# Attention over two batches: query pieces scaled once and copied by transfers between partitions, the own weights' product in front of the first factor's

## The chip, the cores and the metric

One core of a Trainium2 chip runs the whole program. The metric is the device time of one launch in microseconds. The engines are TensorE (PE in the profile), VectorE (DVE), ScalarE (ACT), GpSimd (POOL) and SyncE (SP), which here only issues transfers. "Q" behind an engine's name (SPq, ACTq) means its queue of transfers or its sequencer.

## The reference

The network has three layers. Only the first is touched here:

```python
# x: (32, 64, 512)  ctx: (32, 1601, 512), float32
hc = layernorm(x)                    # 64 tokens a batch
w1, w2, w3 = w_sim[:512], w_sim[512:1024], w_sim[1024:]
Sim = (hc @ w1)[:, :, None] + (ctx @ w2)[:, None, :] \
    + einsum('bid,bjd->bij', hc * w3, ctx) + b_sim
A = softmax(Sim, axis=2)
hq_hat = einsum('bij,bjd->bid', A, ctx)
Batt = softmax(max(Sim, axis=2), axis=1)
hc_bar = einsum('bi,bid->bd', Batt, hc)[:, None, :]
feats = concat([hc, hq_hat, hc * hq_hat, hc * hc_bar], -1)
x = x + feats @ W_qv + b_qv          # W_qv: (2048, 512)
...                                  # a recurrence, then a layer of 8 experts
```

So the query of a token is `hc * w3 + w2`, and a score is its product with a row of the context. The term `hc @ w1` is the same for all context rows of a token, and is dropped from the softmax.

## The kernel before

The attention takes 16 pairs of batches: two batches of 64 tokens make 128 partitions. `bodies` runs a first step (front only), 15 full steps and a last one (back only). A full step with index p does the back of pair p (values, features, output) and the front of pair f = p + 1 (queries, scores, exponentials). Every engine runs its own copy of the step in a written order, and the engines meet only at semaphores.

TensorE's order in a full step (`body` at L447):

- `values`: 13 context positions, the probabilities against the context rows, into the PSUM bank `O`, two column halves (one for each batch). Behind position n = 1 `spread_queries` for two of four blocks; behind n = 5 a small product that spreads `brow` (the softmax over tokens) over all partitions, into `Y`. At n = 1 also the turn of `tcol`.
- `spread_queries` for the other two blocks, then the turn of `tok_rows` (hq_hat) into the bank `T[0]`, which waits for ScalarE to empty `O` (L545).
- the first factor, `product(hqT, 0, ...)`, L408, with w12's first four chunks; it waits for ScalarE's copy `hqT` (L548).
- `own_product`, L416, chunks 0 and 1: hc against weights that depend on the batch, `w0 + w3 * hcb`. GpSimd makes these (`own_weights`, L326 and L329: for each chunk two multiplications and two additions), in two buffers by turns.
- `scores`, L401: 16 blocks of 32 channels, 128 multiplications, four row groups by two column halves at a time, so a block's 32 channels lie in one row group. It needs all context turned (`turned`) and all queries (`q_ready`).
- the second factor `f3` (L408) and own chunks 2 and 3, the turns of the probabilities, the turn of the next pair's tokens.

The layout of the scores asks for each block of 32 query channels at each of the four row groups of 32 partitions. The tokens' transpose `hcT` has channel block e of chunk c on the partitions of group e only. `spread_queries` multiplies it with `spread`, four identity blocks side by side, which copies block e to all four groups, in the PSUM bank `S[:, e]`. ScalarE then scales the copies into `qr` (`queries`, L522): 16 pieces of 128 by 128 for each pair, with `w3R` and `w2R`, columns that hold each block's 32 weights four times. `qr` lies in a part of `x2`, which is not used yet.

VectorE turns the context in 32 by 32 blocks into `ctxT` (L609, L627): the six positions of `ctx_two` one pair ahead, the seven of `ctx_one` in four parts as their transfers land. Between them it does the softmax over tokens (L655 to L670), and `hcb` (L679 and L683), which waits for the brow product. SyncE issues the parts' loads as `values` sets each buffer free (`av_one`), and the two big loads behind its end (`av_done`).

Of the kernel before, what the change touches and what calls it, by code (L numbers as in the profile page):

```python
# [14 lines left out]
P = 128  # L15
# [36 lines left out]
Q = 32  # L52
# [33 lines left out]
def later(p, n):  # L86

    return not isinstance(p, int) or p >= n


def cross_attention(nc, sh, ident, x, ctx, w_sim, b_sim, W_qv, b_qv, x1, x2, ahead):
# [5 lines left out]
    with ExitStack() as stack:  # L97
        def sb(name, shape, dt=F32):
            return stack.enter_context(nc.sbuf_tensor(name, shape, dt))
# [7 lines left out]
        ctx_one = [sb(f"ctx_one{b}", [P, ONE, D]) for b in range(2)]  # L107
        qr = x2[:, 2 * TWO:2 * TWO + C, :].rearrange("p c (e i) -> p (c e) i", e=QUADS)
        w0, w3 = sb("w0", [P, C, D]), sb("w3", [P, C, D])
# [13 lines left out]
        bqv_b = sb("bqv_b", [P, D])  # L123
        spread = sb("spread", [P, P])
        w2R = sb("w2R", [P, DB])
        w3R = sb("w3R", [P, DB])
        bsim_b = sb("bsim_b", [P, 1])
# [29 lines left out]
        wqv_in, w12_in = sem("wqv_in"), sem("w12_in")  # L157
        spread_ready = sem("spread_ready")
        hqT_ready = sem("hqT_ready")
# [12 lines left out]
        xb_ready = sem("xb_ready")  # L172
        q_full, q_ready = sem("q_full"), sem("q_ready")
        hcT_full, hcT_ready = sem("hcT_full"), sem("hcT_ready")
# [51 lines left out]
        def _(sp):  # L226
# [18 lines left out]
            sp.dma_start(w1_b[:], bcast_row(w_sim[0:D])).then_inc(const_in, 16)  # L245
            with nc.allow_non_contiguous_dma(reason="two small weight vectors, a column for each block of 32"):
                for a in range(QUADS):
                    rows = slice(a * Q, (a + 1) * Q)
                    sp.dma_start(w2R[rows, :], w_sim[D:2 * D].rearrange("(k s) -> s k", s=Q)).then_inc(const_in, 16)
                    sp.dma_start(w3R[rows, :], w_sim[2 * D:3 * D].rearrange("(k s) -> s k", s=Q)).then_inc(const_in, 16)  # L250
            sp.dma_start(bsim_b[:], bcast_row(b_sim)).then_inc(const_in, 16)
# [51 lines left out]
        def _(pool):  # L303
# [46 lines left out]

            pool.wait_ge(const_in, 176)
            power(0)
# [3 lines left out]
        def _(pe):  # L356
# [29 lines left out]

            def spread_queries(f, fs, blocks):

                pe.wait_ge(hcT_ready, f + 1)
                for e in blocks:  # L390
                    rows = slice(e * Q, (e + 1) * Q)
                    pe.matmul(S[:, e, :], spread[rows, :], hcT[fs][rows].rearrange("p c i -> p (c i)"),  # L392
                              start=True, stop=True).then_inc(q_full, 1)

            def scores():

                for k in range(DB):
                    for a in range(QUADS):
                        tiles = JT if a * Q < JTAIL else JT - 1
                        for b in range(2):  # L400
                            last = pe.matmul(S[64 * b:64 * b + 64, a, 0:tiles * Q], qr[a * Q:(a + 1) * Q, k, 64 * b:64 * b + 64],  # L401
                                             ctxT[a * Q:(a + 1) * Q, 0:tiles, b, k, :], start=(k == 0), stop=(k == DB - 1))
                return last

            def product(lhsT, w, chunks, start):

                for c in chunks:
                    last = pe.matmul(Y[:], lhsT[:, c, :], w12[:, w + c, :], start=start and c == 0, stop=(w > 0 and c == C - 1))  # L408
                return last

            def own_product(p, s, chunks):

                for c in chunks:
                    pe.wait_ge(wb_ready, 2 * (C * p + c + 1))
                    for b in range(2):
                        last = pe.matmul(Y[64 * b:64 * b + 64, :], hcT[s][:, c, 64 * b:64 * b + 64], wb[:, c % 2, b, :],  # L416
                                         start=False, stop=False)
                    last.then_inc(wb_used, 1)

            def values(p, s, step):  # L420

                pe.wait_ge(hqh_ready, p)
                for n, pos in enumerate(AV_ORDER):
                    for q in range(len(AT_TILES)):
                        if AT_TILES[q][0] == n:
                            pe.wait_ge(t_free[(q + 1) % 2], turn((q + 1) % 2, f"probs{q}", *before(p)) + 1)
                    if n == 2 and step != "last":
                        spread_queries(p + 1, 1 - s, (0, 1))
                    if n == 1:
                        pe.wait_ge(tcol_ready, p + 1)  # L430
                        fill(1, "trow", p, step)
                        pe.transpose(T[1][0:1, 0:P], tcol[:], ident[:]).then_inc(t_full[1], 1)
# [12 lines left out]
                last.then_inc(av_done, 1)  # L445

            def body(p, s, step, loads):  # L447
# [4 lines left out]
                if back:  # L452
                    values(p, s, step)
                    if front:
                        spread_queries(f, fs, (2, 3))
                    pe.wait_ge(hqh_ready, p + 1)
                    turn_tile(0, "hqh", tok_rows, p, step)
                    if first(p):
                        pe.wait_ge(w12_in, 16)
                    pe.wait_ge(hcb_step, p + 1)  # L460
                    pe.wait_ge(hqT_ready, p + 1)
                    product(hqT, 0, range(C), True)
                    own_product(p, s, range(half))
                else:
                    pe.wait_ge(spread_ready, QUADS)
                    turn_tokens(f)
                    spread_queries(f, fs, range(QUADS))
                if front:
                    pe.wait_ge(turned, len(PARTS_ONE) * (f + 1))
                    pe.wait_ge(q_ready, DB * (f + 1))  # L470
                    scores().then_inc(qk_done, 1)
                if back:
                    pe.wait_ge(t_free[0], turn(0, "hqh", p, step) + 1)
                    product(f3, C, range(half), False)
                    own_product(p, s, range(half, C))
# [3 lines left out]
                if back:  # L479
                    product(f3, C, range(half, C), False).then_inc(y_done, 1)  # L480
                if front:
# [20 lines left out]
        def _(act):  # L502
# [13 lines left out]

            def queries(f, e):

                act.wait_ge(q_full, QUADS * f + e + 1)
                for c in range(C):  # L520
                    k = c * QUADS + e
                    act.activation(qr[:, k, :], S[:, e, c * P:(c + 1) * P], ACT.Identity,  # L522
                                   scale=w3R[:, k:k + 1], bias=w2R[:, k:k + 1]).then_inc(q_ready, 1)

            def body(p, s, step, loads):
# [50 lines left out]
                if loads is not None:  # L576
                    tokens(f + 1, s if back else 1)

            for e in range(QUADS):
                rows = slice(e * Q, (e + 1) * Q)  # L580
                act.copy(spread[rows, :].rearrange("p (a s) -> p a s", a=QUADS),
                         ident[rows, None, rows].to_broadcast([Q, QUADS, Q])).then_inc(spread_ready, 1)
            act.wait_ge(const_in, 176)
            norm(0)
# [3 lines left out]
        def _(dve):  # L588
            copy = nc.vector.tensor_copy
            dve.wait_ge(const_in, 176)  # L590

# [1699 lines left out]
```

## Time and profile before

| | |
|---|---|
| median of 3 runs | 1359.72 us (1355.3 to 1359.99) |
| profiled execution, its own time | 1357.04 us |
| its span | 1355.3 us |
| TensorE busy | 1232.2 us, 91% |
| VectorE busy | 730.2 us, 54% |
| GpSimd busy | 707.6 us, 52% |
| ScalarE busy | 337.1 us, 25% |
| attention, first to last pair | to about 680 us of the span |

The span is that of one execution on the chip. A line of a timeline has the start in the span, the time from start to end of the merged instructions, the engine, the line of the kernel, what is written from what, and the number of instructions; one float32 multiplication is recorded as two. In square brackets stands the idle time ahead and what ended it. A duration includes latency: for a run of multiplications the distance from start to start tells what each costs.

### The profile page before, as it was taken

What the parts mean: (1) busy time and instruction counts of PE and PEld (TensorE: products, weight loads), DVE (VectorE), ACT (ScalarE), POOL (GpSimd) and SP (SyncE); (2) the same over time, 40 slices, a digit from 0 to 9 for tenths busy, and PEclk for the clock granted to TensorE, in tenths of its full rate; (3) what the DMA queues carried; (4) which work ended last, traced back from release to release, by engine and by line L of the source; (5) the groups of instructions that cost most, each with busy time, mean ns of one, the idle gap of its engine ahead of it and who ended that gap; (6) DMA issues with size and microseconds to landing.
All of it is one profiled execution on the core that took longest, in us unless ns stands there. A gap on an engine that the chain in (4) does not pass through costs nothing. (4 is left out here: it accounts for less than half of the span.)

```text
span 1355.3 us, 29581 instructions
## 1 busy us (share of the span) xinstructions
PE 1232.2 (91%) x10417; PEld 733.4 (54%) x10418; DVE 730.2 (54%) x1573; ACT 337.1 (25%) x768; POOL 707.6 (52%) x762
## 2 busy tenths in 40 slices
PE   0899999999999999999989699999499999999994
PEld 0444434444443444443457456565378888888883
DVE  4555566555566655566259657777733323323325
ACT  2222233232233232233135211111311111111110
POOL 1055544345543445553139656787398553550872
PEclk9999999999999999999979899999599999999997
DMA  8645554434555444555054567863314443321556
GB/s 284 226 146 200 211 209 154 152 145 176 209 209 178 139 153 159 208 210 193 19 191 142 152 204 273 282 208 103 101 51 144 155 155 131 125 100 56 154 161 188
DMA packets 99376, 225.45 MB, mean 166 GB/s; under 512 B 14152, under 2 KB 30664, under 8 KB 95216
## 3 DMA queue, kind: packets, MB, share of 16 engines
q1 hardware_dynamic: 87872, 189.46, 40.9%
q0 software_dynamic: 10288, 33.57, 7.4%
q10 hardware_dynamic: 1152, 1.57, 0.4%
q8 instruction: 40, 0.66, 0.2%
q14 instruction: 24, 0.20, 0.0%
HBM read 179.21 MB, written 45.35 MB: 166 GB/s over the span
## 5 line engine op out<-in xcount | busy, mean ns | idle before, releaser
L326 POOL TENSOR_TENSOR wb<-w,hcb 128x512 f32<-128x512 f32 x120 | 122.1, 1038 | 315.2 <-DVE hcb L683 292.9
L401 PE MATMUL S<-ctxT,x 32*64 32x416 f32 (+1 forms) x4096 | 185.2, 511 | 15.9 <-DVE ctxT L627 15.9
L401 PEld LDWEIGHTS S<-ctxT,x 32*64 32x64 f32 x4096 | 108.5, 133 | 94.8 <-issue 45.8
L329 POOL TENSOR_TENSOR wb<-wb,w 128x512 f32<-128x512 f32 x120 | 150.0, 1271 | 0.0
L609 DVE STREAM_TRANSPOSE ctxT<-ctx_one 128x1024 f32<-128x1024 f32 (+1 forms) x128 | 115.1, 949 | 13.5 <-DMA ctx_one<-in_ctx_dram 13.2
L436 PE MATMUL O<-ctx_one,probsT 128*64 128x512 f32 (+1 forms) x448 | 110.4, 608 | 0.0
L1929 POOL TENSOR_TENSOR w_low<-w_low,w_high 128x2048 fp32r<-128x2048 f32 x21 | 96.7, 4607 | 1.7
L522 ACT ACTIVATE x<-S,w2R,w3R 128x128 f32<-128x128 f32 x256 | 92.7, 472 | 19.5 <-PE S L392 19.5
L2114 DVE TENSOR_TENSOR f_hL<-f_TH,f_hH 128x512 fp32r<-128x512 f32 x39 | 27.0, 692 | 120.4 <-ACT f_hH L2067 117.3
L634 DVE TENSOR_REDUCE mx<-S 128x1 f32<-128x832 f32 x16 | 16.4, 1025 | 128.1 <-PE S L401 128.1
L1452 PE MATMUL Pb<-WrT,yT 128*32 128x128 f32 x2016 | 69.8, 280 | 13.7 <-DVE yT L1705 13.1
L1473 PE MATMUL Wb<-WoT,yT 128*128 128x512 f32 x128 | 71.8, 643 | 0.0
L2072 ACT ACTIVATE sg<-f_G 128x512 f32<-128x512 f32 x39 | 23.3, 597 | 194.1 <-PE f_G L2014 194.1
L408 PE MATMUL Y<-w,hqT 128*128 128x512 f32 x128 | 58.7, 601 | 12.3 <-ACT hqT L548 12.3
L1452 PEld LDWEIGHTS Pb<-WrT,yT 128*32 128x32 f32 x2016 | 52.3, 111 | 28.5 <-DVE yT L1705 25.7
L2012 PE MATMUL f_Dn<-w_high,f_hH 128*128 x156 | 64.2, 412 | 2.3 <-DVE f_hL L2114 1.6
L2012 PE MATMUL f_U<-w_high,f_xH 128*128 x156 | 64.9, 416 | 0.0
L2012 PE MATMUL f_G<-w_high,f_xH 128*128 x156 | 61.7, 395 | 3.2 <-DVE f_xL L2108 3.2
L1947 POOL CAST w_high<-w_low 128x2048 fp32r<-128x2048 f32 x21 | 39.9, 1898 | 42.9 <-DMA w_low<-_L_ffn_gate_up_proj_dram 22.7
L596 DVE BATCH_NORM_STATS2 stats<-x_sb 128x6 f32<-128x512 f32 x16 | 11.1, 693 | 94.9 <-DMA x_sb<-in_x_dram 82.5
L416 PE MATMUL Y<-wb,hcT 128*64 128x512 f32 x256 | 62.0, 605 | 0.0
L408 PE MATMUL Y<-w,f 128*128 128x512 f32 x128 | 62.0, 606 | 0.0
(286 smaller groups left out, 2497.6 us busy)
## 6 DMA issues: line engine op xcount, KB each, us to landing
ctx_one<-in_ctx_dram SPq DMA_DIRECT2D x64, 512.0 KB, 4.5
x<-in_ctx_dram SPq DMA_DIRECT2D x16, 1536.0 KB
ctx_two<-in_ctx_dram SPq DMA_DIRECT2D x16, 1536.0 KB, 9.4
ctx_one<-in_ctx_dram SPq DMA_DIRECT2D x64, 256.0 KB, 5.5
w_low<-_L_ffn_gate_up_proj_dram POOLq DMA_DIRECT2D x10, 1024.0 KB, 8.1
f_xt<-routed_x SPq DMA_DIRECT2D x39, 256.0 KB
routed_y<-f_yt SPq DMA_DIRECT2D x39, 256.0 KB
w_low<-_L_ffn_gate_up_proj_dram SPq DMA_DIRECT2D x6, 1024.0 KB, 8.0
```

The lines of the kernel that those rows point to most:

```text
L326: pool.tensor_tensor(wb[:, slot, b], w3[:, c], hcb[:, c, b, None].to_broadcast([P, D]), ALU.mult).then_inc(wb_step, 1)
L329: pool.tensor_tensor(wb[:, slot, b], wb[:, slot, b], w0[:, c], ALU.add).then_inc(wb_ready, 1)
L401: last = pe.matmul(S[64 * b:64 * b + 64, a, 0:tiles * Q], qr[a * Q:(a + 1) * Q, k, 64 * b:64 * b + 64], ctxT[a * Q:(a + 1) * Q, 0:tiles, b ...
L408: last = pe.matmul(Y[:], lhsT[:, c, :], w12[:, w + c, :], start=start and c == 0, stop=(w > 0 and c == C - 1))
L416: last = pe.matmul(Y[64 * b:64 * b + 64, :], hcT[s][:, c, 64 * b:64 * b + 64], wb[:, c % 2, b, :], start=False, stop=False)
L436: last = pe.matmul(O[64 * b:64 * b + 64, :], probsT[0:rows, n, 64 * b:64 * b + 64], src[0:rows, i, :], start=(n == 0), stop=(n == JT - 1))
L522: act.activation(qr[:, k, :], S[:, e, c * P:(c + 1) * P], ACT.Identity, scale=w3R[:, k:k + 1], bias=w2R[:, k:k + 1]).then_inc(q_ready, 1)
L609: return dve.transpose(ctxT[:, pos:pos + n, b], src[:, i:i + n, :].rearrange("p t (k r) -> p t k r", r=Q))
L1452: last = pe.matmul(Pb[o * B:(o + 1) * B, 0:P], src[:, c, prev, :], WrT[:, c, o * P:(o + 1) * P], start=(c == 0), stop=(c == C - 1))
L1473: last = pe.matmul(Wb[s][:], yT[s][:, c].rearrange("p t b -> p (t b)"), WoT[:, c, :], start=(c == 0), stop=(c == C - 1))
L1929: pool.tensor_tensor(low, low.bitcast(F32), high[:, e % SLOTS, part].bitcast(F32), ALU.subtract).then_inc(w_parts, 1)
L2012: pe.matmul(bank[:], aH[:, c, :], high[:, slot, part, c, :], start=(c == 0), stop=False)
```

## The change

- `spread`, `spread_queries`, their semaphores and the columns `w2R` and `w3R` go. ScalarE scales the turned tokens directly, in the bank `S[:, 3]`, four pieces of 128 by 128 for each pair (`queries`), into a new tile `q3`, with the columns `w2c` and `w3c` (a column for each chunk). It does so at the end of the step before, behind the copy `hcT`.
- A new function `replicate` has ScalarE issue 16 transfers of 32 partitions by 2 KB from `q3` to `qr`: block e to row group a. It stands behind the exponential of `erow`, ahead of the emptying of `O`. `qr` is laid out with e ahead of c, and the scores index it so and wait for the transfers (`q_in`) in place of `q_ready`.
- In a full and the last step, own chunks 0 and 1 are multiplied ahead of the first factor's product, and open the sum in `Y`.
- The brow product is behind position n = 4, no longer n = 5.
- The eight loads for `w2R` and `w3R` at the start become two.

```diff
             def own_product(p, s, chunks):
...
-                                         start=False, stop=False)
+                                         start=c == 0, stop=False)
...
-                    if n == 2 and step != "last":
-                        spread_queries(p + 1, 1 - s, (0, 1))
...
-                    if n == 5:
+                    if n == 4:
...
                 if back:
                     values(p, s, step)
-                    if front:
-                        spread_queries(f, fs, (2, 3))
                     pe.wait_ge(hqh_ready, p + 1)
                     turn_tile(0, "hqh", tok_rows, p, step)
...
                     pe.wait_ge(hcb_step, p + 1)
+                    own_product(p, s, range(half))
                     pe.wait_ge(hqT_ready, p + 1)
-                    product(hqT, 0, range(C), True)
-                    own_product(p, s, range(half))
+                    product(hqT, 0, range(C))
...
                     pe.wait_ge(turned, len(PARTS_ONE) * (f + 1))
-                    pe.wait_ge(q_ready, DB * (f + 1))
+                    pe.wait_ge(q_in, 16 * QUADS * QUADS * (f + 1))
                     scores().then_inc(qk_done, 1)
...
-            def queries(f, e):
-
-                act.wait_ge(q_full, QUADS * f + e + 1)
+            def queries(f):
+
+                if later(f, 1):
+                    act.wait_ge(q_in, 16 * QUADS * QUADS * f)
                 for c in range(C):
-                    k = c * QUADS + e
-                    act.activation(qr[:, k, :], S[:, e, c * P:(c + 1) * P], ACT.Identity,
-                                   scale=w3R[:, k:k + 1], bias=w2R[:, k:k + 1]).then_inc(q_ready, 1)
+                    act.activation(q3[:, c, :], S[:, QUADS - 1, c * P:(c + 1) * P], ACT.Identity,
+                                   scale=w3c[:, c:c + 1], bias=w2c[:, c:c + 1]).then_inc(q_ready, 1)
+
+            def replicate(f):
+
+                act.wait_ge(q_ready, C * (f + 1))
+                if later(f, 1):
+                    act.wait_ge(qk_done, f)
+                for e in range(QUADS):
+                    for a in range(QUADS):
+                        act.dma_start(qr[a * Q:(a + 1) * Q, e], q3[e * Q:(e + 1) * Q]).then_inc(q_in, 16)
...
                 else:
                     tokens(f, 0)
+                    queries(f)
                 if front:
-                    if later(f, 1):
-                        act.wait_ge(qk_done, f)
-                    queries(f, 0)
-                    queries(f, 1)
+                    replicate(f)
...
-                if front:
-                    queries(f, 2)
-                    queries(f, 3)
...
                 if loads is not None:
                     tokens(f + 1, s if back else 1)
+                    queries(f + 1)
```

## Rows read from the trace of the kernel before

**Rows 1.** The page's part 1: busy time, share of the span and instructions.
```profile
PE 1232.2 (91%) x10417; PEld 733.4 (54%) x10418; DVE 730.2 (54%) x1573; ACT 337.1 (25%) x768; POOL 707.6 (52%) x762
```

**Rows 2.** Timeline, TensorE, one pair: start us, us, engine, line, out<-in, count, idle before.
```profile
299.95 1.08 PE L436 MATMUL O<-ctx_one,probsT 128*64 128x512 f32 x4
...
300.96 1.13 PE L392 MATMUL S<-hcT,spread 32*128 32x512 f32 x4
...
302.02 3.65 PE L436 MATMUL O<-ctx_one,probsT 128*64 128x512 f32 x16
...
305.61 0.48 PE L444 MATMUL Y<-brow,ones 1*128 1x128 f32 x2
...
312.18 1.13 PE L392 MATMUL S<-hcT,spread 32*128 32x512 f32 x4
...
313.24 0.66 PE L365 MATMUL T<-ident,tok_rows 128*128 128x128 f32 x4
...
314.66 3.67 PE L408 MATMUL Y<-w,hqT 128*128 128x512 f32 x8 [0.77 <-ACT hqT L548]
...
318.27 1.94 PE L416 MATMUL Y<-wb,hcT 128*64 128x512 f32 x8
...
320.13 11.42 PE L401 MATMUL S<-ctxT,x 32*64 32x416 f32 x256
...
340.19 1.08 PE L436 MATMUL O<-ctx_one,probsT 128*64 128x512 f32 x4
```

**Rows 3.** The same timeline, VectorE and GpSimd on the own weights.
```profile
302.41 2.35 DVE L609 STREAM_TRANSPOSE ctxT<-ctx_two 128x1024 f32<-128x1024 f32 x2
...
306.13 0.69 DVE L679 TENSOR_TENSOR f<-hcT,Y 128x512 f32<-128x512 f32 x1 [1.37 <-PE Y L444]
...
306.94 0.69 DVE L683 TENSOR_REDUCE hcb<-f 128x8 f32<-128x512 f32 x1
...
307.80 2.04 POOL L326 TENSOR_TENSOR wb<-w,hcb 128x512 f32<-128x512 f32 x2 [18.88 <-DVE hcb L683]
...
314.25 2.50 POOL L329 TENSOR_TENSOR wb<-wb,w 128x512 f32<-128x512 f32 x2
```

**Rows 4.** The same timeline, ScalarE's pieces and who takes erow.
```profile
302.12 2.90 ACT L522 ACTIVATE x<-S,w2R,w3R 128x128 f32<-128x128 f32 x8 [1.13 <-PE S L392]
...
312.30 0.69 ACT L545 ACTIVATE tok_rows<-O,rz 128x512 f32<-128x512 f32 x1 [7.28 <-PE O L436]
...
340.93 0.31 ACT L531 ACTIVATE erow<-erow 1x128 f32<-1x128 f32 x1 [1.25 <-DVE erow L658]
...
341.98 0.23 DVE L665 TENSOR_REDUCE rsum<-erow 1x2 f32<-1x128 f32 x1
```

**Rows 5.** Timeline of the kernel's end, ScalarE's transfer issues.
```profile
1340.56 13.02 ACTq L1884 DMA_DIRECT2D out_dram<-x  x24
```

**Rows 6.** Windows of one pair: busy (instructions) per engine; last PEclk, DMA share, GB/s.
```profile
309.00:311.00 2.00, 2.00 (x12) 0.72 (x10) 1.65 (x2) 0.00 (x0) 2.00 (x2) 1.00 0.91 291
...
315.00:317.00 2.00, 2.00 (x6) 0.87 (x5) 2.00 (x4) 2.00 (x7) 2.00 (x3) 1.00 1.02 436
```

**Rows 7.** The pair's timeline: SyncE's issues of context parts, the last part's turns.
```profile
301.21 6.39 SPq L240 DMA_DIRECT2D ctx_one<-in_ctx_dram  x7
...
314.21 1.31 DVE L609 STREAM_TRANSPOSE ctxT<-ctx_one 128x512 f32<-128x512 f32 x2 [0.40 <-DMA ctx_one<-in_ctx_dram]
...
315.44 1.26 DVE L627 STREAM_TRANSPOSE ctxT<-ctx_one 96x512 f32<-96x512 f32 x2
```

**Rows 8.** Timeline of the start: SyncE's small loads, first turns, first scores.
```profile
2.78 0.42 SPq L249 DMA_DIRECT2D w2R<-in_L_xattn_w_sim_dram  x1
...
7.21 0.49 SPq L251 DMA_DIRECT2D bsim_b<-in_L_xattn_b_sim_dram  x1
...
19.88 6.88 DVE L609 STREAM_TRANSPOSE ctxT<-x 128x1024 f32<-128x1024 f32 x6 [6.20 <-DMA x<-in_ctx_dram]
...
35.49 13.96 PE L401 MATMUL S<-ctxT,x 32*64 32x416 f32 x256 [15.91 <-DVE ctxT L627]
```

More of the change, by code:

```diff
@@ L107, in cross_attention @@
         ctx_one = [sb(f"ctx_one{b}", [P, ONE, D]) for b in range(2)]
-        qr = x2[:, 2 * TWO:2 * TWO + C, :].rearrange("p c (e i) -> p (c e) i", e=QUADS)
+        qr = x2[:, 2 * TWO:2 * TWO + C, :].rearrange("p e (c i) -> p e c i", c=C)
+        q3 = sb("q3", [P, C, P])
         w0, w3 = sb("w0", [P, C, D]), sb("w3", [P, C, D])
@@ L123, in cross_attention @@
         bqv_b = sb("bqv_b", [P, D])
-        spread = sb("spread", [P, P])
-        w2R = sb("w2R", [P, DB])
-        w3R = sb("w3R", [P, DB])
+        w2c, w3c = sb("w2c", [P, C]), sb("w3c", [P, C])
         bsim_b = sb("bsim_b", [P, 1])
@@ L157, in cross_attention @@
         wqv_in, w12_in = sem("wqv_in"), sem("w12_in")
-        spread_ready = sem("spread_ready")
         hqT_ready = sem("hqT_ready")
@@ L172, in cross_attention @@
         xb_ready = sem("xb_ready")
-        q_full, q_ready = sem("q_full"), sem("q_ready")
+        q_ready, q_in = sem("q_ready"), sem("q_in")
         hcT_full, hcT_ready = sem("hcT_full"), sem("hcT_ready")
@@ L245, in _ @@
             sp.dma_start(w1_b[:], bcast_row(w_sim[0:D])).then_inc(const_in, 16)
[L246 to L250, printed above, removed]
+            with nc.allow_non_contiguous_dma(reason="two small weight vectors, a column for each chunk"):
+                sp.dma_start(w2c[:], w_sim[D:2 * D].rearrange("(c p) -> p c", p=P)).then_inc(const_in, 16)
+                sp.dma_start(w3c[:], w_sim[2 * D:3 * D].rearrange("(c p) -> p c", p=P)).then_inc(const_in, 16)
             sp.dma_start(bsim_b[:], bcast_row(b_sim)).then_inc(const_in, 16)
@@ L349, in body @@
                     power(f + 1)
-            pool.wait_ge(const_in, 176)
+            pool.wait_ge(const_in, 80)
             power(0)
@@ L385, in turn_tokens @@
                 last.then_inc(hcT_full, 1)
[L387 to L393, printed above, removed]
             def scores():
@@ L400, in scores, with product @@
                         for b in range(2):
-                            last = pe.matmul(S[64 * b:64 * b + 64, a, 0:tiles * Q], qr[a * Q:(a + 1) * Q, k, 64 * b:64 * b + 64],
+                            last = pe.matmul(S[64 * b:64 * b + 64, a, 0:tiles * Q], qr[a * Q:(a + 1) * Q, k % QUADS, k // QUADS, 64 * b:64 * b + 64],
                                              ctxT[a * Q:(a + 1) * Q, 0:tiles, b, k, :], start=(k == 0), stop=(k == DB - 1))
                 return last
-            def product(lhsT, w, chunks, start):
+            def product(lhsT, w, chunks):
                 for c in chunks:
-                    last = pe.matmul(Y[:], lhsT[:, c, :], w12[:, w + c, :], start=start and c == 0, stop=(w > 0 and c == C - 1))
+                    last = pe.matmul(Y[:], lhsT[:, c, :], w12[:, w + c, :], start=False, stop=(w > 0 and c == C - 1))
                 return last
@@ L460, in body @@
                     pe.wait_ge(hcb_step, p + 1)
+                    own_product(p, s, range(half))
                     pe.wait_ge(hqT_ready, p + 1)
-                    product(hqT, 0, range(C), True)
-                    own_product(p, s, range(half))
+                    product(hqT, 0, range(C))
                 else:
-                    pe.wait_ge(spread_ready, QUADS)
                     turn_tokens(f)
-                    spread_queries(f, fs, range(QUADS))
                 if front:
                     pe.wait_ge(turned, len(PARTS_ONE) * (f + 1))
-                    pe.wait_ge(q_ready, DB * (f + 1))
+                    pe.wait_ge(q_in, 16 * QUADS * QUADS * (f + 1))
                     scores().then_inc(qk_done, 1)
@@ L473, in body @@
                     pe.wait_ge(t_free[0], turn(0, "hqh", p, step) + 1)
-                    product(f3, C, range(half), False)
+                    product(f3, C, range(half))
                     own_product(p, s, range(half, C))
@@ L479, in body @@
                 if back:
-                    product(f3, C, range(half, C), False).then_inc(y_done, 1)
+                    product(f3, C, range(half, C)).then_inc(y_done, 1)
                 if front:
@@ L577, in body @@
                     tokens(f + 1, s if back else 1)
[L579 to L583, printed above, removed]
+                    queries(f + 1)
+            act.wait_ge(const_in, 80)
             norm(0)
@@ L589, in _ @@
             copy = nc.vector.tensor_copy
-            dve.wait_ge(const_in, 176)
+            dve.wait_ge(const_in, 80)
             def norm_stats(f):
```

## The prediction

> **What bounds the kernel now.** I read the page first: TensorE is busy for 91% of the span [rows 1]. The attention is one repeated body for a pair of batches, and the diff stays inside it, so I then read one pair in order of time. It begins anew after 340.19 - 299.95 = 40.24 us [rows 2], and fifteen such pairs make some 604 us. TensorE runs nearly without a gap: values (13 context positions), two spread products, the turn of hq, the first factor's product, the own weights' first half, 11.4 us of scores, then the rest. The one gap named is 0.77 us before the first factor's product [rows 2]. A position of the values with no change of operand shape costs 0.86 us: four of them lie in 305.61 - 302.02 = 3.59, with about 0.15 for the change to the next shape.
>
> A busy TensorE doesn't say what comes next when its work shrinks. So I followed its inputs before the scores, the last place where several chains meet: the own weights (VectorE's hcb, then four GpSimd instructions for each chunk) [rows 3]; the queries on ScalarE [rows 4]; and the turned context, which waits for its transfers [rows 7]. The reader is to see how near each is to 320.13, where the scores start: chunk 1 of the own weights ends at 314.25 + 2.50 = 316.75, the turned context at 315.44 + 1.26 = 316.70.
>
> **What is removed from TensorE.** Two spreads for each pair. The first costs 302.02 - 300.96 = 1.06 us, and the position ahead of it takes 1.01 instead of 0.86, so the path is shorter by 1.06 + 0.15 = 1.21 [rows 2]. The second, also 1.06 us (312.18 to 313.24), is worth nothing: while it runs, ScalarE empties the values' bank (312.30 + 0.69 = 312.99 [rows 4]), and the turn of hq waits for that anyway. Hence the values end at 312.18 - 1.21 = 310.97; with the same steps behind them (0.12 to L545, 0.94 from there to L365) the turn starts at 312.03 and is over by 312.7. Own chunks ahead of the first factor fill the 0.77 gap. If nothing else waited, the scores would start 1.21 + 0.77 = 2.0 us earlier, 15 x 2.0 = 30 us in all.
>
> **What waits next: the own weights.** They now have to be ready before the first factor's product, not behind it. The brow product moves one position forward: 299.95 + 4 x 0.86 + 0.15 = 303.54, and VectorE could have its result at 303.54 + 0.52 = 304.06 (in the rows 306.13 - 305.61 = 0.52). But VectorE is still turning the context for 302.41 + 2.35 = 304.76. So L679 gains only the idle 1.37 us that stands before it, and L683 ends at 307.63 - 1.37 = 306.26 [rows 3]. GpSimd then needs 316.75 - 307.63 = 9.12 us to the end of chunk 1: ready at 315.38. TensorE does chunk 0 at about 312.7 to 313.6, waits some 1.8 us, and does chunk 1 at 315.38 + 0.15 (as L408 follows its release) = 315.53. From there: 0.86 for that chunk, 0.17 for the change of shape, 3.61 for the first factor (318.27 - 314.66) [rows 2]. The scores start at 320.17, against 320.13. The whole 2.0 us is given back to this wait: 0.0 us for each pair, bounds -0.2 and +0.3 for the small steps. GpSimd's later chunks aren't late: its buffers come free when own chunks 0 and 1 are done, now at 319.2 and 320.1 by [rows 2], then at 313.6 and 316.4, and chunks 2 and 3 are needed only behind the scores.
>
> **What is added on ScalarE.** Sixteen query pieces become four, 16 x (2.90 / 8) = 5.8 us against 1.45 [rows 4]. The four sit between the token copy and the exponential of erow, so that moves from 340.93 to about 341.2, plus 0.3 us. The cover is VectorE, which takes its result only at 341.98 in order [rows 4]: cost nothing, and 0.3 us if that cover went. Then 16 transfers are issued. No ScalarE issue is in this stage; the nearest row is the end of the kernel: 24 issues in 13.02 us, 0.54 each [rows 5]. So 16 x 0.54 = 8.7 us, from about 301.2 to 309.9. Behind them on ScalarE is the emptying of the values, wanted at 311.1: 1.2 us spare, plus the 1.8 us of TensorE's new wait, so issues are free up to 0.54 + 3.0/16 = 0.73 us each. The upper bound of an issue I take from SyncE's spell of seven in 6.39 us, 0.91 each with its own waits in it [rows 7]: 14.6 us, which would be 2.9 us late for each pair. I take 0.54, since that row is a run of equal issues. The last is issued 10 us ahead of the scores, so the scores wait for the copies only if these land more than 10 us late.
>
> **What is added to the transfer engines.** Sixteen times 64 KB, 1.05 MB for each pair, beside the context's parts. These are on the way just then, and the engines are at 0.91 to 1.0 of their time [rows 6]. SyncE's transfer issues run 301.21 to 307.6 and on [rows 7]; the parts' 3.4 MB land until 314.21, where VectorE waits 0.40 us for the last [rows 7]. No transfer from SBUF to SBUF is in the trace. Lower bound: 1.05 MB at 436 GB/s, the best row, is 2.4 us. Upper: at 291 GB/s, the row with 2 KB runs like these, 3.6 us [rows 6]. If all of it delays the parts, the last one lands at 316.6 to 317.8, and 316.70 - 314.21 = 2.49 us of turns put the turned context at 319.1 to 320.3. The later parts are issued 1.2 us earlier, which takes perhaps 0.5 off. I take 3.2 us, since the runs are short: 319.9, hidden by a hair; bounds for a pair 0 and +0.3, and beyond them the rival below. For every further us in which the engines are held, the scores start a us later.
>
> The Trainium skill, "DMA: Bandwidth & Descriptors", section "Issuing engines are not separate DMA queues", says that issuing on another engine saves only issue time, as all transfers share the same 16 engines; it speaks against the idea that ScalarE's queue makes these free, and the trace's full engines agree. Its section "Where 436 GB/s comes from" has the fabric's 435 GB/s as the bound between SBUF and SBUF; by that estimate the megabyte costs 2.4 us, the turned context is ready at 319.1, and the pair keeps 0.0 us. By my 3.2 us it is 0.0 too, but with 0.2 us to spare.
>
> **Once only.** At the start, eight small loads for the column weights become two: 7.21 - 2.78 = 4.43 us for eight, so six fewer are 3.3 us on SyncE's queue, and the context's first turns (19.88, which wait for the transfer) come 3.3 us earlier; from there VectorE is busy without a gap until the first scores at 35.49 [rows 8]. I take -3.3. But ScalarE's 16 transfers fall into a full queue there, and the scores may wait for them: bound 0 to +8 (35.49 - 19.88 = 15.6 us is the time they have, 8.7 of it issue, doubled 17.4, behind a start near 17). The last pair has no scores ahead and its own weights come from VectorE: it saves the 0.77 gap. The four spread copies at the start were not on the path.
>
> **The sum.** 15 x (0.0 + 0.1 for near ties) = +1.5, -3.3, -0.8: -2.6 us on the profiled execution's 1357.04, of which 1355.3 is its span: 1354.4. The runs' median, 1359.72, is 2.7 us above the profiled execution, so I forecast 1357. Half a per cent, 6.8 us, is about what this measurement can tell from no change; it is 0.45 us for each pair.
>
> **Rivals.**
> A, the forecast, chance 0.54: TensorE's saving turns into a wait for GpSimd's chunk 1; 1350 to 1363.
> B, 0.18: the copies hold the engines longer than their bytes say, the turned context decides. From 3.4 us of delay on each further us costs 15 us; at 4.3 us it is 0.9 a pair: 1357 + 13 = 1370. For it: the full engines and 32-partition pieces. Against: 1.05 MB is little beside the pair's context of 2 x 1601 x 2 KB = 6.6 MB.
> C, 0.10, the other sign as well: ScalarE's issues take over 0.73 us each beside SyncE's, the values are emptied late, and the scores with them. At 0.91 it is 2.9 us a pair: 1357 + 43 = 1400; at 0.80, 1.1 us: 1374. Against: 0.54 in [rows 5].
> D, 0.12: the wait for chunk 1 is shorter than I think, for example VectorE or GpSimd gets on 0.5 to 2 us earlier, and part of the 30 us remains: at 0.7 us a pair, 1346. Against: in that chain [rows 3] leave no idle time but the 1.37 us.
> E, 0.06: the change does to the pairs nothing at all, but the start gains or loses more than I think (say 8 us): 1350 or 1365.
>
> Faster by over 0.5% (under 1352.9): D, 0.05 of A and 0.02 of E, 0.19. Slower (over 1366.5): 0.14 of B, C, 0.02 of A and 0.01 of E, 0.27. The rest, 0.54. The range 1347 to 1378 leaves out the far ends of C and D; A's own is 1350 to 1363.
>
> **What would show it.** Right: in a pair, L436 runs through 13 positions with only the brow product between them, own chunk 0 starts near 312.7 on this pair's clock, TensorE then waits for GpSimd's L329 about 1.8 us, and the period stays at 40.2 to 40.5. B: the wait ahead of the scores names VectorE's L627, itself behind a transfer, or the transfers of q. C: ScalarE's L545 starts well after the last L436. D: no wait ahead of the second own chunk. The price that I trust least is that of the SBUF copies; the prediction is wrong first if they cost above 3.4 us in the parts' window.

## The result, and the profile after

The changed kernel takes 1390.58 us (median of 4 runs, 1381.26 to 1399.81) against 1358.84 us (4 runs): the ratio is 1.0247, with a 95% interval of 1.0216 to 1.0277. It is slower by 32 us where 1357 was forecast, and lies outside the range of 1347 to 1378.

The page of the changed kernel: part 1, the queue of ScalarE's transfers from part 3, and their group from part 6 (KB each, median us from issue to landing).

```profile
PE 1208.8 (87%) x10289; PEld 733.9 (53%) x10290; DVE 730.3 (53%) x1573; ACT 265.4 (19%) x572; POOL 709.0 (51%) x762
...
q10 hardware_dynamic: 13440, 18.37, 4.8%
...
x<-q ACTq DMA_DIRECT2D x256, 64.0 KB, 6.7
```

TensorE is busy for 1208.8 us, 23.4 less than in [rows 1]: the work did go. The span grew by 31.9 all the same, so TensorE is idle for longer: it waits for something new.

The timeline of one full pair, to be held against [rows 2 to 4] and [rows 7]:

```profile
315.37 0.27 PE L418 MATMUL T<-ident,tcol 128*1 128x128 f32 x1
...
316.33 0.29 ACT L522 ACTIVATE erow<-erow 1x128 f32<-1x128 f32 x1
...
316.49 10.31 ACTq L514 DMA_DIRECT2D x<-q  x16
316.83 5.19 SPq L238 DMA_DIRECT2D ctx_one<-in_ctx_dram  x7
...
319.15 0.48 PE L430 MATMUL Y<-brow,ones 1*128 1x128 f32 x2
...
320.31 0.64 DVE L662 TENSOR_TENSOR f<-hcT,Y 128x512 f32<-128x512 f32 x1
...
326.93 0.69 ACT L534 ACTIVATE tok_rows<-O,rz 128x512 f32<-128x512 f32 x1 [10.31 <-PE O L422]
...
327.68 0.66 PE L361 MATMUL T<-ident,tok_rows 128*128 128x128 f32 x4 [1.02 <-ACT tok_rows L534]
...
328.26 1.08 PE L404 MATMUL Y<-wb,hcT 128*64 128x512 f32 x4
...
328.39 2.50 POOL L325 TENSOR_TENSOR wb<-wb,w 128x512 f32<-128x512 f32 x2
...
330.95 1.08 PE L404 MATMUL Y<-wb,hcT 128*64 128x512 f32 x4 [1.61 <-POOL wb L325]
...
331.96 3.70 PE L396 MATMUL Y<-w,hqT 128*128 128x512 f32 x8
...
334.75 1.30 DVE L592 STREAM_TRANSPOSE ctxT<-ctx_one 128x512 f32<-128x512 f32 x2 [2.50 <-DMA ctx_one<-in_ctx_dram]
335.97 1.26 DVE L610 STREAM_TRANSPOSE ctxT<-ctx_one 96x512 f32<-96x512 f32 x2
...
337.36 11.42 PE L389 MATMUL S<-ctxT,x 32*64 32x416 f32 x256 [1.70 <-DVE ctxT L610]
```

The turn of `tcol` (L418, before L432) is one instruction in each pair, so it serves as the pair's mark, and "behind the mark" means behind its start. Before, it stood at 299.75 and, one pair on, at 340.00:

```profile
299.75 0.27 PE L432 MATMUL T<-ident,tcol 128*1 128x128 f32 x1
```

The scores started 20.38 us behind it, now 21.99. Read backwards from the scores: they wait 1.70 us for VectorE's L610, the last turn of the context. The turn just ahead of it (L592) had waited 2.50 us for its transfer, and starts 19.38 us behind the mark in place of 14.46. The forecast wait for GpSimd's chunk 1 is there as well, 1.61 us, but it isn't the last to end.

The same pair's windows (TensorE's busy time stands first, then PEld, VectorE, ScalarE, GpSimd, the granted clock, the transfer engines' share and GB/s):

```profile
326.00:328.00 2.00, 0.98 (x7) 0.33 (x4) 0.31 (x1) 0.69 (x1) 2.00 (x3) 1.00 1.08 290
328.00:330.00 2.00, 1.34 (x8) 0.29 (x5) 2.00 (x2) 0.59 (x1) 2.00 (x3) 1.00 1.07 293
330.00:332.00 2.00, 1.05 (x5) 0.24 (x5) 1.13 (x3) 0.00 (x0) 2.00 (x2) 1.00 1.08 275
```

The engines are full and move 275 to 293 GB/s, where [rows 6] have 291 and then, with the large loads, 436. From mark to mark, the first fourteen pairs were 40.23 to 40.25 us long before, all alike. Now they are 41.38 to 44.37. With the last, shorter pair (39.80 before, 40.70 now) the mean of fifteen was 40.21 and is 42.29. 15 x 2.08 = 31 us is the whole difference; the layers behind the attention take the same time within 1 us.

Three of the fifteen pairs, of 44.25, 44.37 and 43.87 us, hold another thing. Windows of TensorE alone (busy, granted clock, transfer share, GB/s) at the scores of one of them:

```profile
208.00:212.00 4.00, 2.47 (x32) 0.70 0.99 418
212.00:216.00 4.00, 4.00 (x90) 0.87 0.31 123
```

The granted clock falls from 1.00 to means of 0.70 and 0.87 over 8 us, that is to the lower of its two levels for a part of it. In these three pairs the scores take 13.11 us in place of 11.42, and the stretch from their start to the next mark 21.56 in place of 19.87:

```profile
165.16 13.11 PE L389 MATMUL S<-ctxT,x 32*64 32x416 f32 x256 [2.40 <-DVE ctxT L610]
```

So the lower clock costs 3 x 1.69 = 5 us of the 31, and the other 26 are waiting: the three pairs also waited longer ahead of the scores (2.40, 2.52 and 2.00 us) than most. The other twelve pairs have a mean of 41.82, 1.6 over 40.21.

### The profile page after: what moved, and what is told of

It is laid out like the page before. It is cut to its first block and busy times, and to the rows that moved or that the text cites. A ratio compares the mean times of both kernels' runs of the same rounds, so it can differ in the third digit from the quotient of the medians.

```text
span 1387.2 us, 29337 instructions
## 1 busy us (share of the span) xinstructions
PE 1208.8 (87%) x10289; PEld 733.9 (53%) x10290; DVE 730.3 (53%) x1573; ACT 265.4 (19%) x572; POOL 709.0 (51%) x762
## 5 line engine op out<-in xcount | busy, mean ns | idle before, releaser
L389 PE MATMUL S<-ctxT,x 32*64 32x416 f32 (+1 forms) x4096 | 190.6, 521 | 45.3 <-DVE ctxT L610 27.2
L389 PEld LDWEIGHTS S<-ctxT,x 32*64 32x64 f32 x4096 | 116.4, 136 | 120.7 <-issue 67.4
L592 DVE STREAM_TRANSPOSE ctxT<-ctx_one 128x1024 f32<-128x1024 f32 (+1 forms) x128 | 117.3, 957 | 105.7 <-DMA ctx_one<-in_ctx_dram 105.7
L404 PE MATMUL Y<-wb,hcT 128*64 128x512 f32 x256 | 65.3, 611 | 22.5 <-POOL wb L325 22.5
L1930 POOL CAST w_high<-w_low 128x2048 fp32r<-128x2048 f32 x21 | 39.9, 1902 | 42.6 <-DMA w_low<-_L_ffn_gate_up_proj_dram 22.5
L1997 PE MATMUL f_G<-w_high,f_xL 128*128 x156 | 61.6, 395 | 0.0
L1997 PE MATMUL f_U<-w_high,f_xL 128*128 x156 | 61.5, 394 | 0.0
L1996 PE MATMUL f_G<-w_low,f_xH 128*128 x156 | 61.4, 394 | 0.0
L1997 PE MATMUL f_Dn<-w_high,f_hL 128*128 x156 | 61.2, 392 | 0.0
```

Of the source, the lines that this page charges most:

```text
L592: return dve.transpose(ctxT[:, pos:pos + n, b], src[:, i:i + n, :].rearrange("p t (k r) -> p t k r", r=Q))
L1996: pe.matmul(bank[:], aH[:, c, :], ex.low[:, slot, part, c, :], start=False, stop=False)
L1997: last = pe.matmul(bank[:], aL[:, c, :], high[:, slot, part, c, :], start=False, stop=(c == C - 1))
```

## The experiments

The pairs' periods and the start of the last context turn (L610, L627 in the kernel before) are medians or means over the pairs of a profile. The kernel before ran beside each group: 1354.19 us for the first four, 1354.93 for the next four, 1355.98 for the last three. A time is to be held against the kernel before of its own group; that of the changed kernel (1390.58) was taken beside 1358.84.

**No copies.** The transfers are issued for the first pair only:

```diff
-                if front:
+                if front and not back:
                     replicate(f)
...
-                    pe.wait_ge(q_in, 16 * QUADS * QUADS * (f + 1))
+                    pe.wait_ge(q_in, 16 * QUADS * QUADS)
+                    pe.wait_ge(q_ready, C * (f + 1))
```

> The changed kernel with the 16 query transfers issued for the first pair only; later pairs' scores multiply with the first pair's scaled queries, so the output is not the reference's. Theory T (the copies hold the transfer engines and the context's last part lands late): the wait for VectorE's last turn ahead of the scores goes, the pair falls from about 42.3 us to the 40.2 us that the wait for GpSimd's chunk 1 sets, 1390 - 15 x 2.1 = about 1359. Rival W (the wait for GpSimd's chunk 1 alone costs the 2 us): stays at 1380 to 1390. Rival I (ScalarE's issues hold up the emptying of the values): falls as well, so this run does not tell I from T.

1365.64 us, 1.0085 of before (1.006 to 1.011). The time alone would mislead. In the profile, twelve of fifteen pairs are 39.49 to 40.13 us, three are 41.7 with the clock lowered, and the mean is 40.36. The attention ends 1.4 us later than before. What is longer is the end: from the last expert product to the end of the span 26.8 us against 17.5. With the first pair's queries the output is another, and the tokens take another way through the experts (that this is the cause is argued, not tested), so for this run and the next the pair's period is the measure. The copies, then, carry nearly all of the loss. W falls as the account of the 32 us, but the wait for chunk 1 is exactly where it was forecast:

```profile
PE Y L404 <- POOL wb L325: 24.8, 14, 1.8
```

(columns: us in total, times, longest us) 24.8 us over 14 pairs, and a pair of 40.07 in place of 40.24: what TensorE no longer does is given back to GpSimd, except for 0.17 us.

**Thin copies.** All 16 are issued, but move 64 bytes for a partition:

```diff
-                        act.dma_start(qr[a * Q:(a + 1) * Q, e], q3[e * Q:(e + 1) * Q]).then_inc(q_in, 16)
+                        n = 16 if later(f, 1) else P
+                        act.dma_start(qr[a * Q:(a + 1) * Q, e, 0:1 if later(f, 1) else C, 0:n],
+                                      q3[e * Q:(e + 1) * Q, 0:1 if later(f, 1) else C, 0:n]).then_inc(q_in, 16)
```

> The changed kernel with all 16 transfers still issued for each pair, but from the second pair on each moves 64 bytes for a partition in place of 2 KB (most of the queries are then the first pair's). Theory T (bytes): about 1360, near the run without copies. Rival I (issues on ScalarE, 0.64 us each): the emptying of the values stays as late as in the changed kernel, time 1380 to 1390.

1360.89 us, 1.0044 (1.0025 to 1.0064), again with the long end (27.6 us). The first thirteen pairs are 39.98 to 40.11, the last two 39.88 and 39.48, none with the clock lowered, and the mean is 40.01. The timeline of one:

```profile
309.61 0.69 ACT L536 ACTIVATE tok_rows<-O,rz 128x512 f32<-128x512 f32 x1 [10.29 <-PE O L422]
...
310.35 0.66 PE L361 MATMUL T<-ident,tok_rows 128*128 128x128 f32 x4 [0.99 <-ACT tok_rows L536]
...
310.94 1.08 PE L404 MATMUL Y<-wb,hcT 128*64 128x512 f32 x4
...
313.63 1.08 PE L404 MATMUL Y<-wb,hcT 128*64 128x512 f32 x4 [1.62 <-POOL wb L325]
...
318.27 11.41 PE L389 MATMUL S<-ctxT,x 32*64 32x416 f32 x256
```

ScalarE empties the values just as late as in the changed kernel, behind its 16 issues, and TensorE waits 0.99 us for it. It doesn't matter, since chunk 1 of the own weights comes later still (1.62). The rival of the issues falls. It is bytes.

**The old order of the products, with the copies.**

```diff
...
-                    own_product(p, s, range(half))
                     pe.wait_ge(hqT_ready, p + 1)
                     product(hqT, 0, range(C))
+                    own_product(p, s, range(half))
```

> The changed kernel with own chunks 0 and 1 behind the first factor's product again, transfers kept. Theory T: the scores still wait for the last context part, and the time stays within 5 us of 1390. Rival W: the wait for GpSimd's chunk 1 was the cost, and the time falls by 15 x 1.6 = 24 us to about 1366.

1398.07 us, 1.0311 (1.0262 to 1.036). W is excluded: without its wait the kernel is no faster. T expected within 5 us of 1390, and it is 7.5 slower, or 12 against the kernels before of each group, which T doesn't explain. The last turn starts 20.83 us behind the mark, as in the changed kernel (20.66), and the scores right behind it. But now the waits for chunk 1 and ahead of the scores are one, of up to 3.3 us, and fourteen of the fifteen pairs have a spell at the lower clock; their mean is 43.11. Ten of the spells fall on the scores, each behind a wait of 2.3 to 3.3 us, and cost 1.69 us as above. The other four fall on the first factor's product, and the wait ahead of the scores, which is shorter by as much (0.5 to 1.3 us), hides them:

```profile
417.46 5.37 PE L396 MATMUL Y<-w,hqT 128*128 128x512 f32 x8 [0.77 <-ACT hqT L537]
...
425.35 11.42 PE L389 MATMUL S<-ctxT,x 32*64 32x416 f32 x256 [0.65 <-DVE ctxT L610]
```

By an estimate without the spells on the scores, the pair would be 43.11 - 10 x 1.69 / 15 = 41.98 us here and 42.29 - 3 x 1.69 / 15 = 41.95 in the changed kernel. Seven more spells on the scores are 7 x 1.69 = 12 us, which is the difference. So the order of the products changed nothing but the number of these spells.

**The new order alone**, in the kernel before (spreads kept):

```diff
...
-                    if n == 5:
+                    if n == 4:
...
-                    product(hqT, 0, range(C), True)
-                    own_product(p, s, range(half))
+                    product(hqT, 0, range(C), False)
...
+                    own_product(p, s, range(half))
                     pe.wait_ge(hqT_ready, p + 1)
```

> The kernel before with only the new order: own chunks 0 and 1 ahead of the first factor's product, brow product behind n = 4; spreads and 16 query pieces kept. If the wait for GpSimd's chunk 1 is a real second bound: hcb only 0.86 us earlier, chunk 1 ready at about 315.9 on the pair's clock, scores about 0.5 us later than before, 1359 + 8 = 1367. Rival (order fills the 0.77 us gap and no wait follows): 1359 - 12 = 1347.

1359.5 us, 1.0034 (1.0014 to 1.0054). The pair is 40.71 us, 0.47 more than 40.24; 0.5 was expected. The time is 5.3 over the kernel before beside it, where 8 were expected. TensorE waits for the own weights:

```profile
PE Y L416 <- POOL wb L329: 14.4, 14, 1.1
```

**One own chunk ahead.** As the last, but chunk 1 behind the first factor:

```diff
...
-                    own_product(p, s, range(half))
+                    own_product(p, s, range(1))
                     pe.wait_ge(hqT_ready, p + 1)
                     product(hqT, 0, range(C), False)
+                    own_product(p, s, range(1, half))
```

> The kernel before (spreads on TensorE, no query transfers) with only own chunk 0 ahead of the first factor's product and chunk 1 behind it; brow product behind n = 4. If the wait for chunk 1 is what ate the order's gain, chunk 0 fills the 0.77 us gap and chunk 1 is ready by the time it is wanted: 0.7 us a pair, period 40.24 - 0.7 = 39.5, time 1354 - 11 = 1343. Rival (the order gains nothing for another reason, as the copy of hqT): 1354 to 1359, as with both chunks ahead.

1344.77 us, 0.9921 (0.9892 to 0.995). The pair is 39.59 us, 0.65 less than before, where 0.7 was expected. The order was right by half: the chunk that is ready fills the gap, the other has to stay behind.

**Twelve copies.** Where block and row group agree, the scores read `q3`:

```diff
+                        if a != e:
...
-pe.matmul(S[...], qr[a * Q:(a + 1) * Q, k % QUADS, k // QUADS, ...], ...)
+pe.matmul(S[...], (q3[a * Q:(a + 1) * Q, k // QUADS, ...] if k % QUADS == a else
+                   qr[a * Q:(a + 1) * Q, k % QUADS, k // QUADS, ...]), ...)
```

> The changed kernel with 12 of the 16 transfers: where the block already lies in its row group, the scores read the scaled tile q3 itself. Same result. If the last part's delay goes with the bytes (4.9 us for 16), it falls by 1.2 us, and the usual pair of 41.5 to 41.9 us becomes 40.3 to 40.7: time about 1368 to 1375. Rival (a fixed price of having a second queue beside SyncE's): stays within 5 us of the changed kernel, 1385 to 1395.

1368.67 us, 1.01 (1.0067 to 1.0133). The last turn starts at 19.74 behind the mark, 0.92 less than with 16. The mean pair is 41.03; the eleven pairs without a spell at the lower clock have a mean of 40.77, against 41.82 in the changed kernel. The delay goes with the bytes.

**The large loads held back** until the last part is turned:

```diff
                     sp.wait_ge(av_done, p + 1)
+                    sp.wait_ge(turned, len(PARTS_ONE) * nxt + len(PARTS_ONE))
                     load_two(s, after)
```

> The changed kernel, all 16 transfers, with the next pair's two large context loads issued only when VectorE has turned the last part. Theory O (1.7 of the 4.9 us come from the large loads, which run ahead on some transfer engines while others still carry the last part): the last part lands 1.7 us earlier, 1.5 us off a pair, time about 1366. Rival P (the copies alone hold the last part back): the wait for the last turn stays, 1383 to 1395.

1382.82 us, 1.0203 (1.0173 to 1.0234), where O had 1366 and P 1383 to 1395. One pair:

```profile
313.32 0.27 PE L419 MATMUL T<-ident,tcol 128*1 128x128 f32 x1
...
332.51 1.30 DVE L593 STREAM_TRANSPOSE ctxT<-ctx_one 128x512 f32<-128x512 f32 x2 [2.32 <-DMA ctx_one<-in_ctx_dram]
...
335.13 10.37 PE L390 MATMUL S<-ctxT,x 32*64 32x416 f32 x234 [1.53 <-DVE ctxT L611]
335.18 0.85 SPq L233 DMA_DIRECT2D x<-in_ctx_dram  x2
...
345.67 0.69 DVE L580 BATCH_NORM_STATS2 stats<-x_sb 128x6 f32<-128x512 f32 x1 [10.10 <-DMA x_sb<-in_x_dram]
```

The large loads now start with the scores, and still the last part's turn waits 2.32 us for its transfer. Over all pairs the last turn starts at 20.19, 0.5 earlier, where 1.7 was expected. O accounts for half a microsecond at most, and P for the rest; VectorE's statistics of the next tokens (L580), whose load is held back as well, now come late (a wait of 10.10 us here, 4.70 in the changed kernel's pair), and in three pairs TensorE then waits 1.0 to 1.7 us for the exponentials: this costs something again. The copies themselves hold the parts back.

**A version from both.** Blocks 2 and 3 are spread behind the values, blocks 0 and 1 copied by 6 transfers, one own chunk ahead:

```diff
-                    if n == 2 and step != "last":
-                        spread_queries(p + 1, 1 - s, (0, 1))
...
-                    queries(f, 0)
-                    queries(f, 1)
+                    replicate(f)          # e in (0, 1), a != e
```

> A version from both: blocks 2 and 3 spread by TensorE while ScalarE empties the values (where it costs nothing) and scaled in 8 pieces as before; blocks 0 and 1 scaled once and copied by 6 transfers; own chunk 0 ahead of the first factor, chunk 1 behind; brow product behind n = 4. Six copies at 4.9/16 us delay the last part by 1.8 us, which its 3.4 us of room covers up to scores 1.6 us earlier: period about 38.6, time 1354 - 24 = 1330. Rival (any copies in that window stop TensorE, or the clock falls at the waits): 1345 or more.

1342.66 us, 0.9893 (0.986 to 0.9927), where 1330 was expected. The pairs run from 38.57 to 40.51 but for a last one of 38.16, 39.24 in the mean, where 38.6 was expected. The last turn starts at 17.92, and the scores right behind it: the cover for six copies was just short.

**A filled wait.** The run with the old order, and four multiplications of no use (128x512, into the free bank `O`) ahead of the wait for the scores' inputs:

```diff
                     own_product(p, s, range(half))
+                    if front:
+                        for c in range(C):
+                            pe.matmul(O[:], hqT[:, c, :], w12[:, c, :], start=True, stop=True)
```

> The run with the old order (own chunks 0 and 1 behind the first factor, 16 transfers; mean pair 43.1 us, the granted clock under 1.00 in most pairs) with four 128x512 multiplications of no use in front of the wait for the scores' inputs, 3.5 us of work where TensorE waited 3.3 us. Theory K (an unbroken wait of about 3 us lowers the granted clock for the scores that follow, which costs 1.5 to 2 us): the clock stays at 1.00 through all pairs, mean pair 41.9 to 42.3 us, time about 1383. Rival (the uneven pairs come from late transfers alone): lower clock or not, the mean stays at 43 and the time near 1398.

1405.67 us, 1.0363 (1.0341 to 1.0386). A miss. No spell falls on the scores any longer, but eight fall on the first factor's product, where the run without the filler had four. Its eight instructions take 5.37 us instead of 3.70:

```profile
334.62 0.66 PE L361 MATMUL T<-ident,tok_rows 128*128 128x128 f32 x4 [1.17 <-ACT tok_rows L537]
...
336.04 5.37 PE L396 MATMUL Y<-w,hqT 128*128 128x512 f32 x8 [0.77 <-ACT hqT L540]
...
343.20 3.70 PE L450 MATMUL O<-w,hqT 128*128 128x512 f32 x8
...
346.83 3.48 PE L389 MATMUL S<-ctxT,x 32*64 32x416 f32 x74
```

Ahead of it TensorE had waited 1.17 us and 0.77 us. The pairs with no such spell last 42.6 to 43.1 us (the last one 42.3), the filler overrunning the wait. Theory K, as written, fell: the clock didn't stay at 1.00. The spells on the scores went with the wait ahead of them, but the lower clock doesn't need that wait.

**One block copied.** As the version from both, with 3 transfers and three spreads:

```diff
-                        spread_queries(f, fs, (2, 3))
+                        spread_queries(f, fs, (1, 2, 3))
...
-                for e in range(2):
+                for e in range(1):
                     for a in range(QUADS):
                         if a != e:
                             act.dma_start(qr[a * Q:(a + 1) * Q, e], q3[e * Q:(e + 1) * Q]).then_inc(q_in, 16)
```

> As the version from both, but only block 0 is copied (3 transfers) and blocks 1 to 3 are spread while ScalarE empties the values. Three copies delay the last part by 0.75 us in place of 1.25 to 1.8, TensorE's spread grows by 0.4 us past its cover: pair 38.8 us against 39.2, time about 1337. Rival (ScalarE's 12 pieces, 4.35 us, now end behind the wanted start of the scores): 1343 or more.

1328.97 us, 0.9799 (0.9776 to 0.9822): faster than the kernel before by 27 us, and 62 us under the changed kernel's time. The timeline of one pair:

```profile
302.21 1.13 PE L397 MATMUL S<-hcT,spread 32*128 32x512 f32 x6
302.33 0.69 ACT L568 ACTIVATE tok_rows<-O,rz 128x512 f32<-128x512 f32 x1 [10.08 <-PE O L440]
...
303.28 0.65 PE L370 MATMUL T<-ident,tok_rows 128*128 128x128 f32 x4
...
303.86 1.08 PE L422 MATMUL Y<-wb,hcT 128*64 128x512 f32 x4
...
304.45 4.31 ACT L528 ACTIVATE x<-S,w2R,w3R 128x128 f32<-128x128 f32 x12
...
304.87 3.70 PE L414 MATMUL Y<-w,hqT 128*128 128x512 f32 x8
...
308.11 1.26 DVE L652 STREAM_TRANSPOSE ctxT<-ctx_one 96x512 f32<-96x512 f32 x2
...
308.50 1.08 PE L422 MATMUL Y<-wb,hcT 128*64 128x512 f32 x4
```

The three spreads (six instructions) cost no more than two did, and ScalarE's emptying covers them. The pairs are 38.38 to 38.80 us after a first one of 39.34 (the last 37.95), 38.45 in the mean; the last turn starts at 16.68 and has 0.6 us of room. This is better than the 38.8 us and 1337 expected: the third spread cost nothing, where 0.4 us was expected.

**Twelve blocks in six larger transfers.** `qr` is laid out by the distance between row groups:

```diff
-                for e in range(QUADS):
-                    for a in range(QUADS):
-                        if a != e:
-                            act.dma_start(qr[a * Q:(a + 1) * Q, e], q3[e * Q:(e + 1) * Q]).then_inc(q_in, 16)
+                for j in range(1, QUADS):
+                    n = (QUADS - j) * Q
+                    act.dma_start(qr[0:n, j], q3[P - n:P]).then_inc(q_in, 16)
+                    act.dma_start(qr[n:P, j], q3[0:P - n]).then_inc(q_in, 16)
```

> The run with 12 transfers, the same 12 blocks (0.79 MB) moved as 6 transfers that each span 32 to 96 partitions (qr laid out by the distance of the row groups). If the bytes alone set the price, the last part's turn starts as in the 12 transfer run (19.7 us behind the turn of tcol), 1369. Rival (pieces of 32 partitions reach few ports, or the count of transfers costs): a turn 1 us earlier, ScalarE free 3.8 us earlier, 1360 or less.

1363.36 us, 1.0063 (1.004 to 1.0085), between both expectations (1369, and 1360 or less). The last turn starts at 19.03, 0.7 earlier than with twelve pieces of 32 partitions. Bytes set most of the price, the shape of the pieces some of it.

## Why the prediction was wrong

**TensorE's saving and the wait for chunk 1: right.** TensorE would lose 2.0 us of work and gap, and give it back to GpSimd. The profile after has own chunk 0, a wait of 1.61 us (1.8 forecast), then chunk 1. Without the copies' bytes the pair is 40.07 us, against a forecast of no change from 40.24. Each half was tested by itself: order alone +0.47 us a pair, one chunk ahead -0.65. Rival D, a shorter wait, is excluded.

**ScalarE's issues: priced a little low, free all the same.** 16 issues took 10.31 us, 0.64 each, where [rows 5] gave 0.54. They take 1.6 us longer and end 1.3 later than forecast (11.4 us behind the mark, not 10.15), and hold the emptying of the values up by 0.3. That was under the bound of 0.73 at which it would have cost time; the thin copies show it.

**The step that failed: "I take 3.2 us" for the copies' time on the transfer engines, and "takes perhaps 0.5 off" for the earlier issue of the parts.** The measure is the start of the last turn behind the mark (medians, us), where the kernel before has 15.78:

| kernel | copies of 64 KB | last turn | scores |
|---|---|---|---|
| before | 0 | 15.78 | 20.38 |
| no copies, new order | 0 | 16.53 | 20.22 |
| thin copies | 16 thin | 16.67 | 20.20 |
| one block | 3 | 16.68 | 18.52 |
| from both | 6 | 17.92 | 19.40 |
| twelve, in six transfers | 12 | 19.03 | 20.67 |
| twelve | 12 | 19.74 | 21.22 |
| changed | 16 | 20.66 | 22.04 |

From thin to full copies the turn moves by 20.66 - 16.67 = 3.99 us for 1.05 MB, that is 263 GB/s. It is below the 291 GB/s of [rows 6] which I took as the lower end. By the Trainium skill's 435 GB/s as the bound for copies within SBUF ("DMA: Bandwidth & Descriptors", "Where 436 GB/s comes from") the estimate is 2.4 us; here the measurement decides. The second term has the wrong sign. Without copies, but with TensorE ahead of its old timetable, the last turn starts 0.75 us later than before, not 0.5 us earlier. In this kernel the large loads, too, are issued about 1.2 us earlier, and fall onto the last part's tail; holding them back gave 0.5 us in the changed kernel. That the two are the same effect is likely and not shown; what causes the 0.75 us stays open.

Together the last turn came 3.99 + 0.89 = 4.88 us later than in the kernel before (the thin copies stand at 0.89). The prediction's ready time of 319.9 is 316.70 + 3.2: its sum doesn't take the 0.5 off that the text names, so 3.2 was forecast (2.7 with it). The room was 20.38 - 15.78 - 1.26 = 3.34 us. 4.88 - 3.34 = 1.5 us a pair, with 0.1 from turn to scores, makes the 1.6 us of the twelve undisturbed pairs. So it was rival B, "the turned context decides", with 0.18 given to it. Its place and its rule (a microsecond later for each one more) were right. Its price at 4.3 us was right too; its size was not, 4.9.

**The granted clock, in no part of the prediction.** 5 of the 32 us are spells at the lower level: in three pairs of the changed kernel and fourteen with the old order, none in the kernel before and the version with one block once the first values are under way. They came in all kernels with 12 or 16 full copies, but also in three pairs without copies, and not with thin ones or six. On the scores they came only behind a wait of 2.0 us or more, but waits of 2.03, 2.21, 2.25 and 2.66 us had none behind them. Without copies, they came behind waits of 0.79 and 1.8 us, which most of the other pairs have as well, with no fall. What decides on them stays open.

**The start: -3.3 forecast, -0.2 got.** The first scores start at 34.21 us in place of 35.49, but wait for the copies, whose issues (18.21 to 28.45) fall among the loads of the weights, as I had feared:

```profile
34.21 13.73 PE L389 MATMUL S<-ctxT,x 32*64 32x416 f32 x256 [18.07 <-DMA x<-q]
...
51.92 1.25 DVE L592 STREAM_TRANSPOSE ctxT<-ctx_two 128x1024 f32<-128x1024 f32 x1 [1.35 <-DMA ctx_two<-in_ctx_dram]
```

The six loads fewer brought the first turns of the context only 1.94 us forward (17.94 against 19.88), so the turned context was ready at 33.49, and the copies took 0.7 of that. The large loads behind are then late in turn (1.35 us at 51.92). The lower clock, from 52.6 to 59.4 us in place of 54.3 to 57.8, took some 0.5 us of the values that follow. By the first mark (58.09 against 58.32) nearly all is given back.

## What to carry to other kernels

Before work is moved from the bounding engine to the transfer engines, ask whether these are idle in the stretch in which the moved bytes must pass; a mean share over the kernel hides that they are full just there. Price the room as well: from each input's last event to the start of what needs it. Bring forward only the part of a product whose operand is already there, and put work that must stay on the bounding engine under a wait that it has anyway: the spreads cost 1.2 us at one place and nothing at the other.

## What the runs showed of the hardware

- Copies within SBUF in pieces of 32 partitions by 2 KB, beside loads that fill the engines, cost 0.25 us for 64 KB (16 of them 3.99 us, 263 GB/s). The first few cost less, in kernels that keep two or three of the spreads: six moved the last turn by 1.25 us, three by 0.01. Twelve blocks in pieces of 32 to 96 partitions moved the last turn by 19.03 - 16.67 = 2.4 us for 0.79 MB, 333 GB/s.
- Three multiplications over 32 rows each, in three row groups, lasted 1.13 us, the same as two: the merged row at 302.21 has six instructions, [rows 2] have four.
- TensorE's granted clock fell to the lower level for 3.4 us of a pair. It cost 1.69 us on the scores (13.11 in place of 11.42) and 1.67 us on the first factor's product (5.37 in place of 3.70), and came in 3 of 15 pairs in one kernel and in 14 in another. Ahead of it stood one wait of 2.0 to 3.3 us, or two: of 1.0 to 1.4 and 0.8 us, or of 0.8 and 1.8 us. The same waits stood in other pairs with no fall.
